# Routing of the second expert stage in groups of 1, 1, 1, 2 and 3 batches in place of 1, 1, 2, 2 and 2

## The chip, the cores and the metric
The kernel runs on one core of one Trainium2 chip. The time is device microseconds of one execution. Of the kernel before there are three: 1153.13, 1153.15 and 1154.1 us, median 1153.15 us. A further execution was recorded by the profiler.

## The reference, cut to what matters
The input x has 8 batches of 512 tokens with 128 channels, so 4096 tokens. Four layers follow each other, each added to x:

```
x = x + attention(layernorm(x))
x = x + experts(layernorm(x))        # first expert stage
x = x + delta_rule(layernorm(x))
x = x + experts(layernorm(x))        # second expert stage: the change is here
```

The experts are eight networks 128 -> 512 -> 128 with a GELU. Each token is sent to one of them:

```
logits = (x @ w_red) @ normalised(wg).T       # 8 numbers per token
idx    = argmax(softmax(logits)); score = softmax(logits)[idx]
out    = (gelu(x @ w1[idx] + b1[idx]) @ w2[idx] + b2[idx]) * score
```

## The kernel before, in words
x stays in SBUF as 32 tiles of 128 tokens x 128 channels, four tiles to a batch. The function `experts(..., f)` is built twice, with f = 0 and f = 1. In the second one (f = 1) it does the routing for all eight batches first, and only then the expert networks.

Routing sorts the tokens by expert. Each token's normalised row (with its own number behind it, 129 words) is written by an indirect DMA to a row of `xs_dram`, in the area of its expert. Its place there is the number of tokens that chose the same expert before it. The work goes by groups of batches, `GROUPS`, of 1, 1, 2, 2 and 2 batches. For a group the steps are:

- `moments(b)`, DVE: mean and variance of the four tiles of a batch, 4 statistics and 4 aggregations.
- `variance(g)` DVE, `deviation(g)` ACT (square root), `deviation(g)` DVE (reciprocal and one correcting step): 1/deviation of all tiles of the group.
- `normalize(g)`, DVE: `xa` from `x`, one instruction per tile.
- `turn(b)`, PE: four transposes of `xa` to PSUM; `turned(b)`, ACT: the copy `rT` to SBUF; `logits(b)`, PE: for each tile a product with the gate's weights.
- `choose(g)`, DVE: five instructions, from the logits to the one-hot `oh`.
- `ranks(g)`, PE: counts the tokens of each expert before each token; it starts from the group before's totals, which `counted(g - 1)`, ACT, copies to `cnt`.
- `place(g)`, DVE: three instructions, to the whole-number places `pos`.
- GpSimd (POOL): one indirect DMA per tile, from L1430, as soon as `place(g)` is done; four for a batch.

The groups are tied to each other by the running totals. Each engine works off its own list in the order in which it is written: DVE's and ACT's orders are written out by hand, PE takes group by group all turns, then all logits, then the ranks.

Behind the last `place`, DVE computes the tables (`tables()`: which expert each of the 24 tiles of 256 rows has, and from which row it is read). From its first result (`end_done`) ACT issues eight fills of 129 KB (L1496), which put blank rows behind each expert's last token. From its last result (`texp_done`) SP loads the weights of the first three tiles (L1375 to L1381). Then SP waits until all scatters and all fills have landed, and loads the rows of the first tiles (`f_xs`, L1390). The waits are these:

```
            for q in range(SLOTS - 1):
                weights(0, q, f > 0)
            sp.wait_ge(s["scat_done"], 16 * TT * (B // 2 + 1) + 16 * NT * f)
            sp.wait_ge(s["scat_odd"], 16 * TT * (B // 2 - 1))
            sp.wait_ge(s["fill_done"], 16 * E * (f + 1))
```

After that PE works through 24 tiles (transpose L1782, up L1792, down L1802, transpose back L1813), POOL scatters the results (L1438), SP loads them back in token order (L1413), and DVE adds them to x (L1717).

Of the kernel before, what the change touches and what calls it, by code (L numbers as in the profile page):

```python
# [14 lines left out]
B, T, C = 8, 512, 128  # L15
H, HD = 16, 8
TT = T // P
NT = B * TT
# [25 lines left out]
NC2 = ST // P  # L44
EPS_G = 1e-4
GROUPS = ((0, 1), (1, 2), (2, 4), (4, 6), (6, B))
SINGLE = tuple((b, b + 1) for b in range(B))
AREA = B * T + ST
IDLE = 2 * SPAN
# [1224 lines left out]
def experts(nc, x, xs_dram, ys_dram, s, keep, f, w_red, wg, w1, b1, w2, b2, out):  # L1274
    with ExitStack() as ctx:
# [18 lines left out]
        area = keep["area"]  # L1294
        tile_at = keep["tile_at"]
        k_at = keep["k_at"]
        GR = GROUPS if f else SINGLE
        NG = len(GR)
        FIRST = 0 if f else NG - 1
        GB, CB = B * f, (B - 1) * f  # L1300
# [49 lines left out]
        def tiles(g):  # L1350

            return slice(TT * GR[g][0], TT * GR[g][1])

        def width(g):

            return TT * (GR[g][1] - GR[g][0])

# [88 lines left out]
        def _(act):  # L1446
            def deviation(g):
                act.wait_ge(s["rstd_step"], 6 * (GB + g) + 1)
                if f == 0:
                    act.activation(rstd[:, 2, tiles(g)], rstd[:, 1, tiles(g)], ACT.Ln).then_inc(s["rstd_step"], 1)  # L1450
                    act.wait_ge(s["rstd_step"], 6 * (GB + g) + 2)
                    act.activation(rstd[:, 3, tiles(g)], rstd[:, 2, tiles(g)], ACT.Exp, scale=-0.5)\
                        .then_inc(s["rstd_step"], 1)
                else:
                    act.activation(rstd[:, 2, tiles(g)], rstd[:, 1, tiles(g)], ACT.Sqrt).then_inc(s["rstd_step"], 1)

            def turned(b):
                act.wait_ge(s["rT_ps"], B * f + b + 1)
                if b >= 2:
                    act.wait_ge(s["lg_ps"], B * f + b - 1)  # L1460
                act.activation(rT[:, b % 2, :], (bA, bB)[b % 2][:, :], ACT.Copy).then_inc(s["rT_sb"], 1)

            def counted(g):
                n = width(g)
                act.wait_ge(s["rank_ps"], GB + g + 1)
                act.activation(cnt[:, g % 2, :], rank_bank(g)[:, E * n:E * n + E], ACT.Copy).then_inc(s["cnt_sb"], 1)

            if f == 0:
                deviation(NG - 1)
                turned(B - 1)  # L1470
            else:
                deviation(0)
                turned(0)
                deviation(1)
                counted(0)
                turned(1)
                counted(1)
                deviation(2)
                turned(2)
                turned(3)  # L1480
                deviation(3)
                counted(2)
                turned(4)
                turned(5)
                deviation(4)
                counted(3)
                turned(6)
                turned(7)
            act.wait_ge(s["lg_step"], 4 * (GB + NG))
# [41 lines left out]
        def _(dve):  # L1531
            def moments(b):
                n0 = 2 * NT * f + 2 * TT * b
                four = range(TT * b, TT * b + TT)
                for i in four:
                    dve.bn_stats(stats[:, i, :], x[:, i, :]).then_inc(s["stat_done"], 1)  # L1536
                for k, i in enumerate(four):
                    dve.wait_ge(s["stat_done"], n0 + k + 1)
                    dve.bn_aggr(mv[:, i, :], stats[:, i, :]).then_inc(s["stat_done"], 1)

            def variance(g):
                dve.wait_ge(s["stat_done"], 2 * NT * f + 2 * TT * GR[g][1])
                dve.tensor_scalar(rstd[:, 1, tiles(g)], mv[:, tiles(g), 1], EPS_LN, None, ALU.add)\
                    .then_inc(s["rstd_step"], 1)
# [14 lines left out]
                dve.wait_ge(s["rstd_step"], n0 + 6)  # L1559
                dve.tensor_tensor(rstd[:, 0, at], rstd[:, 2, at], rstd[:, 3, at], ALU.mult).then_inc(s["rstd_ready"], 1)  # L1560

            def normalize(g):
                dve.wait_ge(s["rstd_ready"], GB + g + 1)
                for i in range(NT)[tiles(g)]:
                    dve.tensor_scalar(xa[:, i, 0:C], x[:, i, :], mv[:, i, 0:1], rstd[:, 0, i:i + 1],  # L1565
                                      ALU.subtract, ALU.mult).then_inc(s["xnf_done"], 1)

            def choose(g):

                at, n, n0 = tiles(g), width(g), 4 * (GB + g)  # L1570
                lg = bH[:, g % 4, 0:E * n].rearrange("p (i e) -> p i e", e=E)
                dve.wait_ge(s["lg_ps"], B * f + GR[g][1])
                dve.tensor_reduce(top[:, at], lg, AX.X, ALU.max).then_inc(s["lg_step"], 1)
                dve.wait_ge(s["lg_step"], n0 + 1)
                dve.tensor_tensor(lgx[:, at, :], lg, top[:, at].unsqueeze(2).broadcast_to([P, n, E]), ALU.subtract)\
                    .then_inc(s["lg_step"], 1)
                dve.wait_ge(s["lg_step"], n0 + 2)
                dve.scalar_tensor_tensor(hit[:, at, :], lgx[:, at, :], 0.0,
                                         pref[:, :].unsqueeze(1).broadcast_to([P, n, E]), ALU.is_equal, ALU.mult)\
                    .then_inc(s["lg_step"], 1)  # L1580
                dve.wait_ge(s["lg_step"], n0 + 3)
                dve.tensor_reduce(first[:, at], hit[:, at, :], AX.X, ALU.max).then_inc(s["lg_step"], 1)
                dve.wait_ge(s["lg_step"], n0 + 4)
                dve.tensor_tensor(oh[:, at, :], pref[:, :].unsqueeze(1).broadcast_to([P, n, E]),
                                  first[:, at].unsqueeze(2).broadcast_to([P, n, E]), ALU.is_equal)\
                    .then_inc(s["oh_done"], 1)
# [51 lines left out]
            if f == 0:  # L1638
                moments(B - 1)
                variance(NG - 1)  # L1640
                deviation(NG - 1)
                normalize(NG - 1)
                choose(NG - 1)
                place(NG - 1)
            else:
                moments(0)
                variance(0)
                deviation(0)
                normalize(0)
                moments(1)  # L1650
                variance(1)
                deviation(1)
                choose(0)
                normalize(1)
                place(0)
                moments(2)
                choose(1)
                moments(3)
                variance(2)
                place(1)  # L1660
                deviation(2)
                normalize(2)
                moments(4)
                moments(5)
                variance(3)
                choose(2)
                place(2)
                deviation(3)
                normalize(3)
                moments(6)  # L1670
                moments(7)
                variance(4)
                choose(3)
                place(3)
                deviation(4)
                normalize(4)
                choose(4)
                place(4)
            tables()
# [1040 lines left out]
```

## Time and profile before

| what | value |
|---|---|
| median of the runs | 1153.15 us |
| profiled execution, its own time | 1146.83 us |
| its span, first to last instruction | 1145.0 us |
| PE busy | 851.1 us (74%) |
| DVE busy | 760.2 us (66%) |
| POOL busy | 562.0 us (49%) |
| ACT busy | 535.8 us (47%) |
| mean granted TensorE clock | 0.849 of full |

The span is the time between the first and the last instruction; the execution's own time has 1.83 us more around it. Busy shares are means over very different stages. All times of rows are microseconds from the span's start. The second expert stage begins at about 956.8.

### The profile page before, as it was taken

The page shows a single profiled execution, that of the slowest core. Times are in us where ns is not written, and L with a number is a line of the kernel's source. Part 1 is how long each engine was busy: PE and PEld are TensorE (multiplying, and loading weights), DVE is VectorE, ACT ScalarE, POOL GpSimd, SP SyncE. Part 2 cuts the span into 40 slices and gives each one's busy share as a digit, 9 for nine tenths or more (in the row PEclk, how much of TensorE's full clock was granted, in tenths as well). Part 3 has the DMA queues.
Part 4 walks back from the last instruction along what each step waited for, and adds up shares of the span by engine and source line. Part 5 has one row for each costly group of instructions (what it writes and reads, how often), then busy time and mean ns, then how long its engine had stood idle before and what let it go on. Part 6 is the DMA issues. An engine that isn't in the chain of part 4 may idle for free. (4 is left out here: it accounts for less than half of the span.)

```text
span 1145.0 us, 26725 instructions
## 1 busy us (share of the span) xinstructions
PE 851.1 (74%) x9326; PEld 632.7 (55%) x9326; DVE 760.2 (66%) x1722; ACT 535.8 (47%) x1219; POOL 562.0 (49%) x698
## 2 busy tenths in 40 slices
PE   3678888888888753999188999467867674629992
PEld 2455555555555542888124786156655563528881
DVE  7577687786877741223364889999999997512224
ACT  4577667586675721454055220255555531115450
POOL 4456557575665631445550010277777841533442
PEclk9998888797887965999688999878889886559996
DMA  5342241432414004566338400000020110155665
GB/s 162 112 157 91 68 159 41 134 98 70 159 41 134 9 14 139 168 202 187 100 58 109 74 1 0 0 1 0 0 73 0 37 38 7 40 157 163 196 195 165
DMA packets 129207, 101.80 MB, mean 89 GB/s; under 512 B 20640, under 2 KB 116832, under 8 KB 129056
## 3 DMA queue, kind: packets, MB, share of 16 engines
q1 hardware_dynamic: 120080, 87.27, 27.6%
q0 software_dynamic: 5120, 10.53, 2.6%
q10 hardware_dynamic: 3904, 2.61, 0.7%
q8 instruction: 68, 1.11, 0.4%
q14 instruction: 35, 0.29, 0.1%
HBM read 57.98 MB, written 35.45 MB: 82 GB/s over the span
## 5 line engine op out<-in xcount | busy, mean ns | idle before, releaser
L795 DVE TENSOR_SCALAR a_mag<-a_pS 128x1024 int32<-128x1024 int32 (+1 forms) x192 | 179.9, 949 | 66.6 <-PE a_pS L1154 65.7
L552 ACT ACTIVATE a_pw<-a_mag,a_eps_a 128x1024 f32<-128x1024 f32 (+1 forms) x192 | 175.0, 936 | 56.7 <-DVE a_mag L795 50.7
L1438 POOL DMA_INDIRECT ys_dram<-f_yo,f_who x96 | 92.1, 960 | 133.6 <-DVE f_yo L1703 116.9
L415 POOL TENSOR_TENSOR a_pw<-a_pw,a_decay 128x256 f32<-128x256 f32 x128 | 93.4, 730 | 105.2 <-ACT a_pw L552 104.5
L1154 PE MATMUL a_pS<-a_qf,a_kf 64*64 64x192 bf16 (+3 forms) x1536 | 112.2, 272 | 5.2 <-DVE a_mag L795 4.5
L1513 ACT ACTIVATE f_hs<-f_bH,f_bs 128x256 f32<-128x256 f32 x192 | 75.4, 475 | 69.0 <-PE f_bH L1792 69.0
L2613 PE MATMUL d_c<-d_pb_p,ident 128*128 128x256 f32 x256 | 72.3, 452 | 42.1 <-POOL d_pb_p L2096 42.1
L1186 PE MATMUL a_pOff<-a_pw,a_vo 128*18 128x64 f32 x3584 | 95.9, 241 | 1.2 <-issue 1.2
L1792 PE MATMUL f_bH<-f_xsT,f_w1s 128*128 128x256 f32 x384 | 95.6, 394 | 0.0
L1688 DVE TENSOR_SCALAR f_ysT<-f_bY,f_bs 128x256 f32<-128x256 f32 x48 | 23.2, 483 | 108.2 <-PE f_bY L1802 108.2
L1802 PE MATMUL f_bY<-f_hs,f_w2s 128*128 128x256 f32 x384 | 90.8, 379 | 0.0
L2613 PEld LDWEIGHTS d_c<-d_pb_p,ident 128*128 128x128 f32 x256 | 58.5, 232 | 56.3 <-issue 40.8
L1154 PEld LDWEIGHTS a_pS<-a_qf,a_kf 64*64 64x64 bf16 x1536 | 65.8, 116 | 30.7 <-DVE a_mag L795 7.6
L2613 PE MATMUL d_c<-d_pb_d,ident 128*128 128x256 f32 (+1 forms) x256 | 64.6, 419 | 21.7 <-POOL d_pb_d L2096 21.7
L2090 POOL TENSOR_TENSOR d_pb_p<-d_Q,d_s_sb 128x512 f32<-128x512 f32 x32 | 37.5, 1171 | 83.1 <-ACT d_s_sb L2198 83.1
L1186 PEld LDWEIGHTS a_pOff<-a_pw,a_vo 128*18 128x18 f32 x3584 | 68.6, 110 | 15.9 <-issue 11.4
L1792 PEld LDWEIGHTS f_bH<-f_xsT,f_w1s 128*128 128x128 f32 x384 | 72.4, 199 | 8.9
L1802 PEld LDWEIGHTS f_bY<-f_hs,f_w2s 128*128 128x128 f32 x384 | 69.4, 190 | 7.5
L2613 PEld LDWEIGHTS d_c<-d_pb_d,ident 128*128 128x128 f32 x256 | 53.1, 220 | 33.1 <-POOL d_pb_d L2096 24.6
L363 POOL TENSOR_TENSOR a_vo<-a_vd,a_reach 128x1008 f32<-128x1008 f32 (+6 forms) x56 | 66.0, 1194 | 1.1 <-issue 1.1
L1703 DVE COPY f_yo<-f_bO 128x256 f32<-128x256 f32 x48 | 20.4, 425 | 62.0 <-PE f_bO L1813 62.0
L2194 ACT ACTIVATE d_G<-d_c,d_g_ahead 128x64 f32<-128x64 f32 x64 | 24.1, 376 | 71.2 <-DVE d_og L2431 71.2
(395 smaller groups left out, 1837.9 us busy)
## 6 DMA issues: line engine op xcount, KB each, us to landing
parts_scratch<-a_parts SPq DMA_DIRECT2D x32, 384.0 KB, 3.4
f_w1s<-in_L_ffn_w_dram SPq DMA_DIRECT2D x48, 256.0 KB
f_w2s<-in_L_ffn_w_dram SPq DMA_DIRECT2D x48, 256.0 KB
a_kf<-parts_scratch SPq DMA_DIRECT2D x16, 512.0 KB, 4.8
a_qf<-parts_scratch SPq DMA_DIRECT2D x16, 512.0 KB, 5.6
f_xs<-xs_dram SPq DMA_DIRECT2D x48, 129.0 KB, 2.3
parts_scratch<-a_parts SPq DMA_DIRECT2D x16, 256.0 KB, 2.4
xs_dram<-blank ACTq DMA_DIRECT2D x16, 129.0 KB, 4.2
```

The lines of the kernel that those rows point to most:

```text
L363: pool.tensor_tensor(vo[:, vo_at(j, j + 1):vo_at(j, j + 1) + n, :, :], vd[:, k, j, :, :].unsqueeze(1).broadcast_to([P, n, NP, 18]), reach[ ...
L415: pool.tensor_tensor(own, own, decay[:, k, m, hf:NP:2, :], ALU.mult)\
L552: act.activation(pw[:, n % 4, 0:N], mag[:, n % 3, 0:N], ACT.Square, bias=eps_a[:, 0:1])\
L795: dve.tensor_scalar(mag[:, n % 3, 0:2 * N].bitcast(I32).rearrange("p (l t) -> p l t", l=2), pS[:, 2 * (n % 2):2 * (n % 2) + 2, 0:N].bitcas ...
L1154: ins = pe.matmul(pS[lo:hi, 2 * (n % 2) + Q // 2, at:at + L * (end - first)], kf[lo:hi, k, p, L * m:L * m + L], qf[lo:hi, k, p, L * first: ...
L1186: ins = pe.matmul(pOff[lo:hi, L * i:L * i + L], vo[:, vo_at(m, i), p, :], wi, start=False, stop=(m == NM - 2), skip_group_check=True)
L1438: pool.indirect_dma_start(ys_dram[f][:, :], bass.IndirectOffsetOnAxis(ap=who[:, q, a:a + 1], axis=0), yo[:, q, a, :], None).then_inc(ys_ou ...
L1513: ins = act.activation(hs[:, q % 2, n, :], bH[:, 2 * (q % 2) + n // 2, ST * (n % 2):ST * (n % 2) + ST], ACT.Gelu, bias=bs[:, q, n:n + 1])
L1792: ins = pe.matmul(bH[:, 2 * (q % 2) + n // 2, ST * (n % 2):ST * (n % 2) + ST], w1s[:, q, P * n:P * n + P], xsT[:, q % 2, :], start=True, s ...
L1802: ins = pe.matmul(bY[:, 0:ST], w2s[:, q, n, :], hs[:, q % 2, n, :], start=(n == 0), stop=(n == NF - 1))
L2090: pool.tensor_tensor(po[:, 0:8], Q[:, :, :, bass.ds(c, 1)].rearrange("p k j c -> p k (j c)").unsqueeze(3) .broadcast_to([P, HD, CH, HD]), ...
L2613: ins = pe.matmul((c5, c6)[a][:, 0:64 * chunks].rearrange("p (c x) -> p c x", x=64), ident[:, :], po[:, k], start=(k == 0), stop=(k == 15))
```

## The change
The second expert stage takes its groups from a new tuple. `normalize` gets a batch beside the group. The batches of a group are normalised one at a time, some before and some after the `place` of the group before it. The orders on DVE and ACT are rewritten for it. The first expert stage still has a single batch here, and does the same instructions as before.

```
+ROUTED = ((0, 1), (1, 2), (2, 3), (3, 5), (5, B))
-        GR = GROUPS if f else SINGLE
+        GR = ROUTED if f else SINGLE
ACT, from the third deviation on:
                 turned(1)
+                deviation(2)
                 counted(1)
-                deviation(2)
                 turned(2)
-                turned(3)
                 deviation(3)
                 counted(2)
+                turned(3)
                 turned(4)
-                turned(5)
                 deviation(4)
                 counted(3)
+                turned(5)
                 turned(6)
                 turned(7)
DVE:
-            def normalize(g):
+            def normalize(g, b):
                 dve.wait_ge(s["rstd_ready"], GB + g + 1)
-                for i in range(NT)[tiles(g)]:
+                for i in range(TT * b, TT * b + TT):
...
                 moments(2)
+                variance(2)
                 choose(1)
+                deviation(2)
+                normalize(2, 2)
+                place(1)
                 moments(3)
-                variance(2)
-                place(1)
-                deviation(2)
-                normalize(2)
                 moments(4)
-                moments(5)
                 variance(3)
                 choose(2)
+                deviation(3)
+                normalize(3, 3)
                 place(2)
-                deviation(3)
-                normalize(3)
+                normalize(3, 4)
+                moments(5)
                 moments(6)
                 moments(7)
                 variance(4)
                 choose(3)
+                deviation(4)
+                normalize(4, 5)
                 place(3)
-                deviation(4)
-                normalize(4)
+                normalize(4, 6)
+                normalize(4, 7)
                 choose(4)
                 place(4)
```

## Rows read from the trace of the kernel before

**Rows 1.** Chain of waits, routing's end to the kernel's end: start, us, what
```profile
1009.56 14.37 issue
1023.93 0.67 PE f_bA L1782 x2
...
1025.15 0.66 PE f_bA L1782 x2
...
1116.42 1.73 PE f_bH L1792 x8
```

**Rows 2.** Waits of SP's queue: who waited for what, total us, times, longest
```profile
SPq L1397 <- DMA xs_dram<-blank: 3.3, 1, 3.3
SPq L1386 <- DMA xs_dram<-f_xa,f_pos: 0.4, 1, 0.4
```

**Rows 3.** Timeline of SP and ACT, after the last places: start, us, instruction
```profile
1007.00 8.25 ACTq L1496 DMA_DIRECT2D xs_dram<-blank  x8
...
1016.56 0.62 SPq L1381 DMA_DIRECT2D f_bs<-bT  x1
1021.73 1.57 SPq L1390 DMA_DIRECT2D f_xs<-xs_dram  x2
```

**Rows 4.** Timeline of POOL, first and last scatter of the last group
```profile
1006.08 0.96 POOL L1430 DMA_INDIRECT xs_dram<-f_xa,f_pos  x1 [0.94 <-DVE f_pos L1599]
...
1014.94 0.96 POOL L1430 DMA_INDIRECT xs_dram<-f_xa,f_pos  x1 [0.30 <-issue]
```

**Rows 5.** Line L1430, all 32 scatters of the stage: duration ns min/median/max, first and last start
```profile
L1430 POOL DMA_INDIRECT xs_dram<-f_xa,f_pos x32: 956/962/1095, 968.1 to 1014.9; - x32
```

**Rows 6.** Busy time by stretch: us, busy by engine, clock, DMA share, GB/s
```profile
1015.00:1016.00 1.00, 0.00 (x0) 0.00 (x0) 0.00 (x0) 0.00 (x0) 0.90 (x1) 0.50 0.96 260
...
1019.00:1020.00 1.00, 0.00 (x0) 0.00 (x0) 0.00 (x0) 0.00 (x0) 0.00 (x0) 0.50 0.73 200
...
1021.00:1022.00 1.00, 0.00 (x0) 0.00 (x0) 0.00 (x0) 0.00 (x0) 0.00 (x0) 0.50 0.04 7
```

**Rows 7.** Timeline of DVE, groups of one batch
```profile
959.41 1.11 DVE L1565 TENSOR_SCALAR f_xa<-x,f_mv,f_rstd 128x128 f32<-128x128 f32 x4
...
964.30 0.19 DVE L1573 TENSOR_REDUCE f_top<-f_bH 128x4 f32<-128x32 f32 x1 [0.87 <-PE f_bH L1738]
...
970.18 0.19 DVE L1573 TENSOR_REDUCE f_top<-f_bH 128x4 f32<-128x32 f32 x1 [1.88 <-PE f_bH L1738]
...
972.95 0.17 DVE L1599 CAST f_pos<-f_pos_f 128x4 int32<-128x4 f32 x1
```

**Rows 8.** Timeline of DVE, fourth group (two batches) and its places
```profile
991.62 0.22 DVE L1573 TENSOR_REDUCE f_top<-f_bH 128x8 f32<-128x64 f32 x1 [2.13 <-PE f_bH L1738]
...
994.36 0.23 DVE L1595 TENSOR_TENSOR f_p_at<-f_bO,f_oh 128x64 f32<-128x64 f32 x1 [1.50 <-ACT cnt L1466]
...
994.96 0.20 DVE L1551 RECIPROCAL f_rstd<-f_rstd 128x8 f32<-128x8 f32 x1
...
996.00 2.14 DVE L1565 TENSOR_SCALAR f_xa<-x,f_mv,f_rstd 128x128 f32<-128x128 f32 x8
1002.65 0.22 DVE L1573 TENSOR_REDUCE f_top<-f_bH 128x8 f32<-128x64 f32 x1 [4.51 <-PE f_bH L1738]
...
1005.63 0.17 DVE L1599 CAST f_pos<-f_pos_f 128x8 int32<-128x8 f32 x1
```

**Rows 9.** Timeline of PE: logits and ranks
```profile
965.44 0.64 PE L1752 MATMUL f_bY<-area,one_row 1*128 1x40 f32 x2 [1.18 <-DVE f_oh L1584]
...
988.15 3.43 PE L1738 MATMUL f_bH<-w_gate,f_rT 128*128 128x8 f32 x16
```

**Rows 10.** Busy time by stretch: last two groups; then the expert networks' first microseconds
```profile
990.00:1003.00 13.00, 8.15 (x43) 7.31 (x42) 4.97 (x23) 2.66 (x4) 9.11 (x11) 0.50 0.15 48
...
1030.00:1031.00 1.00, 1.00 (x6) 0.84 (x5) 0.00 (x0) 1.00 (x4) 0.00 (x0) 0.86 0.00 0
```

**Rows 11.** Result scatters of the expert networks (L1438): us to landing
```profile
DMA to landing us min/median/max: 2.2/2.6/3.6
```

## What the change will do to the time: the prediction
> **What bounds the kernel now.** I read the chain of waits first, then the waits of SP, then the timelines of the second expert stage. The chain shows that from 1023.93 us on PE works almost without a pause to 1116.42 + 1.73 = 1118.15, and that before it stand 14.37 us, from 1009.56, in which no engine computes anything on the path [rows 1]. The output part behind it is not touched. So whatever moves the first row load at 1021.73 [rows 3] moves the end by as much; the routing counts only through it.
>
> The reader should ask what that first row load waited for. SP was through with the weights at 1016.56 + 0.62 = 1017.18 [rows 3]. Then it waited 3.3 us for the last fill, to 1020.5, and after that another 0.4 us for a scatter [rows 2]. So the last scatter landed at about 1020.9, and the load followed 0.85 us later (1021.73 - 1020.9). Fill and scatter were nearly equally late. The last scatter had started on POOL at 1014.94 [rows 4], so it took L = 6.0 us to land. The result scatters of the same kind, of nearly equal size, take 2.2 at best, 2.6 in the median and 3.6 at most [rows 11]. The 6.0 has a reason in view: weights, fills and scatters run together, the DMA engines are at 0.96 of their time and more at 1015, still at 0.73 at 1019, and at 0.04 once the last of it is in, at 1021 [rows 6].
>
> **What the change does, part by part.** I call F the time by which the last `place` ends earlier; before, it ends at 1005.63 + 0.17 = 1005.80 [rows 8]. Number of instructions: one batch's tiles keep the same number of statistics, normalisations, transposes and logits. There are still five groups, so `choose`, `place`, `ranks`, `deviation` keep their number too; only their widths differ. All of the gain is order: a group's chain DVE, ACT, PE, DVE no longer waits for the normalisation of two batches at once, and DVE's idle time before `choose` is used once less.
>
> The path after the change, from the first place where it differs:
>
> - `choose(1)` starts at 970.18 as before [rows 7]: the new `variance(2)` lies in front of it, in the 1.88 us in which DVE waits for the logits [rows 7]. So this edit costs nothing; without that cover it would cost 0.2.
> - `choose` with four tiles lasts 1.14 (964.30 to the ranks on PE at 965.44) [rows 7, 9], `deviation` 1.04 (994.96 to 996.00), from the reciprocal to the normalisation [rows 8], one batch's normalisation 1.11 [rows 7]. From 970.18 that gives 973.45 for the normalised batch 2. Its square root lies beside `choose(1)`.
> - From the end of a single normalisation (959.41 + 1.11 = 960.52) to `choose` are 3.78 us [rows 7]: `choose(2)` at 977.25. Moments of batches 3 and 4 and `variance(3)`, some 2.4 us, lie inside these 3.8.
> - `choose(2)` 1.14, `deviation(3)` 1.04, batch 3's normalisation 1.03 (half of 2.14, less the tail), `place(2)` 0.60 (994.36 to 994.96) [rows 8], batch 4's normalisation 1.11: 982.2. From the end of a pair's normalisation (996.00 + 2.14) to `choose` are 4.51 us [rows 8]: `choose(3)` at 986.7.
> - `choose(3)` with eight tiles 1.3 (five instructions of 0.22 in place of 0.19) [rows 7, 8], `deviation(4)` 1.04, batch 5 1.03, `place(3)` 0.60, batches 6 and 7 2.14: 992.8. `place(3)` here waits for the counts, which PE and ACT make under the deviation and batch 5's normalisation.
> - Then 4.51 as for a pair, and one batch's logits more, half of 3.43 = 1.7 [rows 9]: `choose(4)` at 999.0.
> - From `choose` to the end of `place`: with eight tiles in the last group 3.15 (1002.65 to 1005.80). Eight tiles cost about 0.5 more than four: 3.34 from 991.62 to the instruction behind the last of `place` at 994.96, against 2.94 from 970.18 to 972.95 + 0.17, and that end lies some 0.1 later than the other [rows 7, 8]. So twelve 3.65: the last `place` ends at 1002.65.
>
> That makes F = 3.15. The steps on DVE are each taken to the end of the last instruction or to the start of another engine's; the next instruction on DVE itself starts a few hundredths earlier. An estimate of 0.04 for each of the eleven handovers gives 3.6. I take **F = 3.3**.
>
> What the change takes back: the last group has 12 scatters in place of 8. Eight take 1014.94 - 1006.08 = 8.86 from the first start to the last, 1.266 each [rows 4], so four more put the last start 5.06 us further behind the last `place`. POOL must be free by then: the fourth group's places end at about 990.6 (992.8 less the 2.14), its eight scatters take 10.1 to 1001.0, and the first of the last group is ready at 1002.5 + 0.28 = 1002.8. It is free, by 1.8 us. The last scatter thus starts at 1014.94 - 3.3 + 5.06 = 1016.7, **later than before by 1.8 us**.
>
> What then goes with F: tables, fills and weights all hang on the last `place`, so the fills that landed at 1020.5 land at about 1017.2, plus what four scatters more in that stretch cost them. A scatter moves 128 rows of 129 words, 66 KB; at the 260 GB/s of this stretch [rows 6] that is 0.25 us, 1.0 for four. So the fills are in by 1018.2 at the latest, and are no longer last. And the DMA engines run empty before the last scatter needs them: the tail that ended at 1021.1 ends at 1017.8 to 1018.8. The last scatter therefore lands after L = 2.2 to 3.6 [rows 11]. I take the median, 2.6, since some tail is left. Row load: 1016.7 + 2.6 + 0.85 = 1020.15 against 1021.73. In one formula, the row load comes earlier by F - 5.06 + (6.0 - L) = 3.3 - 5.06 + 3.4 = **1.6 us**. Bounds: with L = 2.2 and F = 3.6, 2.3 earlier; with L = 3.6 and F = 3.15, 0.5 earlier; with L = 6.0, 1.8 later. The sum for the profiled execution, 1146.83 with a span of 1145.0, is 1145.2. The median of the runs is 6.3 above the profiled one, and I move it by the same difference: 1153.15 - 1.6 = 1151.5.
>
> On L the trace's shortest is 2.2 [rows 11]. The Trainium skill, "DMA: Bandwidth & Descriptors", section "Anatomy of one DMA", gives a DMA from GpSimd a fixed 2.0 us, mostly the receipt of the write, and bytes by 436 GB/s: an estimate of 2.15 us for 66 KB. The trace's 2.2 agrees; its 6.0 under full load does not follow from that rule. By it the sum would be 2.05 us, and 1151.1.
>
> A cost that I put at nothing: the normalisations of batches 6 and 7 now run on DVE while POOL issues the fourth group's scatters. The 32 scatters last 956 to 1095 ns, with the median at 962, although many of them already lie beside normalisations [rows 5]. So I see no loss; even 0.2 us for each of eight would not use up the 1.8 us by which POOL is free. The Trainium skill, "SBUF — State Buffer", section "SBUF: two separate sides", says that certain DVE instructions lock GpSimd out of a shared port, so that it can't write the descriptors of its DMAs. That would speak against this order; the durations of this trace do not show it.
>
> **Rivals.**
>
> A. The forecast: 1.6 us earlier, 1151.5. For it: the load's last two waits end within 0.4 us of each other, and both come with full DMA engines [rows 2, 6].
>
> B. The scatter tail decides on the other side. The landing time stays at 6.0, because the twelve scatters' packets still queue behind weights and fills, with 0.26 MB more to move. Then POOL's 5.06 us outweigh F: 1.8 us later, 1154.9. It decides from L = 4.2 on (5.06 - 3.3 = 1.8 less than 6.0). For it: 6.0 is the only number for this spot. Against: the engines are nearly idle by 1021 [rows 6], and everything else moves forward.
>
> C. The front gains less than the steps say: the chain through PE, ACT and DVE has four handovers with new neighbours, and DVE may be late for `choose(4)`. With F = 0 and L = 2.6 the load is 1.7 later: 1154.8. The break is at F = 1.7. Against: DVE has 4.51 us of idle time before the last `choose` [rows 8] and the terms are all measured.
>
> D. TensorE's clock rises in the last group. Routing runs at 0.50, that is 1.2 GHz, from 990 to 1003 [rows 10]. In the expert networks PE runs unbroken from 1025.15 [rows 1], and the granted clock rises within 1030 to 1031 (mean 0.86) [rows 10], some 5.1 us later. The new last group keeps PE at work from about 990 to 999. If the clock doubled at about 996, the rest of the logits and the ranks would take half: 1.5 us less, so 3.1 earlier in all, 1150.0. Against: 997 to 1002.6 was also nearly unbroken and stayed at 0.50, with logits of only eight columns [rows 8 to 10].
>
> That the change does nothing isn't a case: the orders are different on three engines. That all of F arrives (1149.8) is ruled out by POOL: the last scatter can't be in before 1016.7 + 2.2.
>
> **How the numbers follow.** A 0.62, B 0.12, C 0.12, D 0.08, and 0.06 for gains or losses of the later stage's clock that I can't place. The likeliest is A: 1151.5; its own range is 1150.4 to 1152.8. The range to 8 in 10 takes in part of B, C and D: 1149.7 to 1154.6. A difference can be told from no change only beyond 0.2%, 2.3 us. A lies mostly within it; a third of A, nearly all of D and half of the rest are faster than that: 0.20 + 0.07 + 0.03 = 0.30. B and C are slower by less than 2.3 in most of their course; a third of their 0.24 and a little of the rest are slower than that: 0.10. The same: 0.60.
>
> **What would show it.** In the changed kernel: last `place` ends at 1002.2 to 1002.7; last scatter starts at 1016.3 to 1017 and POOL idles between the fourth and last group; SP's longest wait after the weights is for a scatter and no longer for a fill; the first row load is at 1019.5 to 1020.9; PE's granted clock is 0.50 in all of the routing. A scatter that lands after more than 4.2 us proves B, a last `place` after 1004.1 proves C, a clock above 0.50 before 1003 proves D. The forecast is wrong if the row load moves by the amount said and the end doesn't.

## The result, and the profile after

The changed kernel takes 1150.68 us in the median of 17 runs (1149.16 to 1154.53), the kernel before 1153.68 in the median of 17 runs beside them (1151.43 to 1156.16). The ratio is 0.9976 with a 95% interval of 0.9966 to 0.9985, that is 2.8 us faster (1.7 to 3.9). Run again twice beside the experiments, the same kernel gave 0.9968 and 0.9970, so 3.7 and 3.5 us. The forecast was 1.6 us faster, with 1149.7 to 1154.6 as the range. The sign was right and the time lies in the range; 1.6 itself lies just below the measured interval, and one term of the sum was well off.

The profiled execution of the changed kernel has 1151.33 us of its own (span 1149.5), 0.65 above its median. That of before had 1146.83, which is 6.3 to 6.9 us *below* the median of its runs. So the two profiles can't be set beside each other as they stand: the changed kernel's is 4.5 us longer although the kernel is faster. Of these 4.5 us, 2.8 are there before the second expert stage begins (959.61 against 956.78), in code that the change does not touch, and 2.1 come behind the first row load (125.4 us to the end of the span against 123.3). I therefore took two more profiles of the kernel before, unchanged, and compare with them too.

The second expert stage starts with the first statistics on DVE. Here that row, before and then after (timeline of DVE; start, us, instruction, in brackets the idle time before it and what ended it). All times "into the stage" below are counted from it: 956.78 before, 959.61 after.

```profile
956.78 0.87 DVE L1536 BATCH_NORM_STATS2 f_stats<-x 128x6 f32<-128x128 f32 x4 [0.32 <-PEq L1839]
```

After, timeline of DVE: `choose` of groups 2, 3 and 4 (L1574) and the last place (L1596, L1600).

```profile
959.61 0.87 DVE L1537 BATCH_NORM_STATS2 f_stats<-x 128x6 f32<-128x128 f32 x4 [0.32 <-PEq L1843]
...
979.90 0.19 DVE L1574 TENSOR_REDUCE f_top<-f_bH 128x4 f32<-128x32 f32 x1 [0.77 <-PE f_bH L1742]
...
989.53 0.23 DVE L1574 TENSOR_REDUCE f_top<-f_bH 128x8 f32<-128x64 f32 x1 [1.55 <-PE f_bH L1742]
...
1001.73 0.26 DVE L1574 TENSOR_REDUCE f_top<-f_bH 128x12 f32<-128x96 f32 x1 [6.15 <-PE f_bH L1742]
...
1005.13 0.26 DVE L1596 TENSOR_TENSOR f_p_at<-f_bY,f_oh 128x96 f32<-128x96 f32 x1 [1.98 <-PE f_bY L1761]
...
1005.71 0.17 DVE L1600 CAST f_pos<-f_pos_f 128x12 int32<-128x12 f32 x1
```

These answer to [rows 8]. The three `choose` are 20.29, 29.92 and 42.12 us into the stage; the prediction had 20.47, 29.92 and 42.22. The last place ends at 1005.71 + 0.17 = 1005.88, 46.27 into the stage, where before it was 1005.80 - 956.78 = 49.02: 2.75 earlier, forecast 3.3.

Part of the missing half microsecond shows in the last ranks. Timeline of PE: they end at 1003.95 + 0.74 = 1004.69, and DVE goes on at 1005.13, 0.44 later. On most handovers of this stage that gap is 0.04.

```profile
1003.95 0.74 PE L1761 MATMUL f_bY<-f_oh,ones 128*128 128x96 bf16 x12
```

After, timeline of POOL, first and last scatter of the last group, answering to [rows 4]: POOL was idle for 2.60 us before the last group (0.94 before) and starts the last scatter 60.43 into the stage.

```profile
1006.16 0.96 POOL L1431 DMA_INDIRECT xs_dram<-f_xa,f_pos  x1 [2.60 <-DVE f_pos L1600]
...
1020.04 0.96 POOL L1431 DMA_INDIRECT xs_dram<-f_xa,f_pos  x1 [0.31 <-issue]
```

After, timeline of ACT and SP, answering to [rows 3]: the eight fills, then the DMAs of the weights, then the first row load.

```profile
1007.09 11.90 ACTq L1497 DMA_DIRECT2D xs_dram<-blank  x8
...
1016.87 0.01 SPq L1382 DMA_DIRECT2D f_bs<-bT  x1
...
1023.31 0.01 SPq L1382 DMA_DIRECT2D f_bs<-bT  x1
1024.12 2.75 SPq L1391 DMA_DIRECT2D f_xs<-xs_dram  x3
```

Nobody had forecast this. Before, SP was through with the weights at 1017.18, 60.40 into the stage, and waited 3.7 us more. After, it sends the last of the weights only at 1023.31, 63.70 in, and the row load follows 0.81 later without any wait for a fill or a scatter. The chain of waits names SP's own instructions there (start, us, what):

```profile
1017.57 0.70 SPq L1373
1018.27 0.69 issue
```

What takes 0.7 us is, each time, a single small instruction. The rows of the weights' line show it, first before, then after (durations in ns min/median/max, first and last start). The same MOVE lasts 45 at most in the one and 700 in the other; the fills on ACT last 11.90 in place of 8.25. I call these hold-ups.

```profile
L1375 SPq MOVE f_w1s<-in_L_ffn_w_dram x3: 29/29/45, 1010.3 to 1015.4; - x3
```

```profile
L1376 SPq MOVE f_w1s<-in_L_ffn_w_dram x3: 5/45/700, 1010.4 to 1020.4; - x3
```

Then the two kernels' row loads: 64.95 into the stage before, 64.52 after. By these two profiles the change would bring 0.4 us. The median says 2.8.

### The profile page after: what moved, and what is told of

The parts are those of the page before. It is cut to its first block and busy times, and to the rows that moved or that the text cites. A ratio compares the mean times of both kernels' runs of the same rounds, so it can differ in the third digit from the quotient of the medians.

```text
span 1149.5 us, 26726 instructions
## 1 busy us (share of the span) xinstructions
PE 853.0 (74%) x9326; PEld 630.0 (55%) x9326; DVE 761.6 (66%) x1722; ACT 536.1 (47%) x1219; POOL 560.9 (49%) x698
```

## The experiments

Each time is the median of its runs, each ratio against the kernel before in the same job. That kernel's median was 1153.32 (27 runs) for the first four, 1155.63 (23) for the next four, 1156.92 (29) for the last four.

**The change again**, three profiles in all with the one further down. No edit.

> The changed kernel once more, for a second profile of it and its time beside the next three on the same chip. In its first profile the stage starts at 959.61 us in place of 956.78, before anything that the change touches, so all times are taken from the stage's start (its first statistics on DVE). My theory, that the last place comes about 3 us earlier and the last scatter lands in under 4.2 us: first row load 62 to 64 us after the stage's start (before: 64.95), time 1.5 to 3 us under the kernel before. Rival, that POOL's longer last group gives the time back: row load at 65 or later and no gain. In the first profile SP and ACT had single instructions of 0.7 us while the weights were issued; if that belongs to the change it comes again, if it is chance it is gone.

1149.40, ratio 0.9968 (0.9954 to 0.9982), so 3.7 us faster (2.1 to 5.3), more than expected. The profiled execution took 1153.71, 4.3 above that median. Its row load, 64.72 us into the stage, lies between what was expected (62 to 64) and the rival (65 or later), and the hold-ups came again: the fills last 11.22 us. SP waited for a scatter now, and shortly (waits of SP: who for whom, total, times, longest; then the timeline of SP; the stage starts at 960.09 here):

```profile
SPq L1387 <- DMA xs_dram<-f_xa,f_pos: 0.3, 1, 0.3
```

```profile
1024.81 2.75 SPq L1391 DMA_DIRECT2D f_xs<-xs_dram  x3
```

**Only the order**: groups 1, 1, 2, 2, 2 as before, but rows normalised batch by batch around the places. In the third group, for instance (against the changed kernel):

```
-ROUTED = ((0, 1), (1, 2), (2, 3), (3, 5), (5, B))
+ROUTED = ((0, 1), (1, 2), (2, 4), (4, 6), (6, B))
...
+                variance(2)
                 deviation(2)
                 normalize(2, 2)
                 place(1)
+                normalize(2, 3)
```

> Only the order is changed: groups of 1, 1, 2, 2 and 2 batches as before, but of each pair one batch is normalised before the place of the group in front and one behind it. Steps from the rows of before: last place 2.7 us earlier; POOL has no idle time left before the last eight scatters, so its last scatter starts only 0.6 us earlier. Theory 1 (the backlog of weights, fills and scatters on the DMA engines sets the row load, all of which hangs on the last place): about 2.5 us faster, as much as the whole change, so the new groups add nothing. Theory 2 (POOL's last scatter plus a fixed 6 us sets it): 0.6 us faster.

1154.17, ratio 1.0014 (0.9998 to 1.0030): both expectations missed. The profiled execution took 1161.13, 7.0 above that median, so its row load is not the usual one. Timelines of PE, ACT, POOL, DVE and SP (the stage starts at 960.21; the 15.94 are the eight fills):

```profile
996.40 0.45 PE L1761 MATMUL f_bO<-f_oh,ones 128*128 128x64 bf16 x8
1000.14 0.18 ACT L1467 ACTIVATE cnt<-f_bO 128x8 f32<-128x8 f32 x1 [8.02 <-remote]
1001.38 0.96 POOL L1431 DMA_INDIRECT xs_dram<-f_xa,f_pos  x1 [2.76 <-DVE f_pos L1600]
...
1010.37 0.17 DVE L1600 CAST f_pos<-f_pos_f 128x8 int32<-128x8 f32 x1
1011.75 15.94 ACTq L1497 DMA_DIRECT2D xs_dram<-blank  x8
...
1032.09 2.75 SPq L1391 DMA_DIRECT2D f_xs<-xs_dram  x3
```

The fourth group's ranks end at 996.85, and ACT, which makes the counts from them, starts only at 1000.14: a pause of 3.29 us in which ACT does nothing and everything that needs the counts stands, POOL too. The last place ends 50.33 into the stage instead of near 46, and the row load is at 71.88. The pause does not explain that row load: the last scatter starts at 60.16 and has landed at 62.47, and what holds the load are the fills, which are issued over 15.94 us (8.25 in the first profile of before) and land at 71.03. So this profile shows why the last place missed its mark, but not why the median shows no gain.

**Only the groups**: 1, 1, 1, 2, 3, but each group normalised in one piece behind the place, as before. In the last group, for instance (against the changed kernel):

```
 ROUTED = ((0, 1), (1, 2), (2, 3), (3, 5), (5, B))
...
                 choose(3)
+                place(3)
                 deviation(4)
                 normalize(4, 5)
-                place(3)
                 normalize(4, 6)
                 normalize(4, 7)
```

> Only the groups are changed: 1, 1, 1, 2 and 3 batches, and each group is normalised in one piece behind the place of the group in front, as in the kernel before. Steps from the rows: last place 0.8 us later than before, last scatter starts 5.8 us later, so with a landing in 2.6 us the row load and the time are 2.4 us later than before. If the groups were what gives the gain, it would be faster by 1 us or more.

1154.40, ratio 1.0007 (0.9996 to 1.0019). No gain, but not the loss of 2.4 us that was expected. Timeline of PE, DVE and SP (the stage starts at 956.68):

```profile
997.88 5.12 PE L1742 MATMUL f_bH<-w_gate,f_rT 128*128 128x8 f32 x24
...
1004.38 0.26 DVE L1574 TENSOR_REDUCE f_top<-f_bH 128x12 f32<-128x96 f32 x1 [7.46 <-PE f_bH L1742]
...
1007.96 0.17 DVE L1600 CAST f_pos<-f_pos_f 128x12 int32<-128x12 f32 x1
1026.13 2.75 SPq L1391 DMA_DIRECT2D f_xs<-xs_dram  x3
```

Here too a pause: the last logits end at 1003.00, DVE goes on at 1004.38, 1.38 later. The last place ends at 51.45, and the row load is at 69.45; in the usual execution of before (below) they are near 52.3 and 68.9.

**Four groups**: 1, 2, 2, 3, batch by batch as in the change; the orders on DVE and ACT follow.

```
-ROUTED = ((0, 1), (1, 2), (2, 3), (3, 5), (5, B))
+ROUTED = ((0, 1), (1, 3), (3, 5), (5, B))
```

> Four groups of 1, 2, 2 and 3 batches, normalised batch by batch around the places: one whole pass through the chain of engines less. Steps from the rows: last place 7.9 us earlier than before, POOL's last scatter starts 2.9 us earlier (POOL is busy almost without a gap from the second group on). If the chain's passes and POOL's queue are what counts, with a landing of 2.6 us: about 6 us faster than before. If the landing stays at 6 us: 2.7 us faster. If the routing's end doesn't matter: no difference.

1146.99, ratio 0.9951 (0.9936 to 0.9966): 5.7 us (3.9 to 7.4) faster than before, as expected, and the lowest ratio but one here (0.9950 with late weights, below, is the same within the noise). The same timelines (the stage starts at 955.39):

```profile
996.49 0.26 DVE L1572 TENSOR_REDUCE f_top<-f_bH 128x12 f32<-128x96 f32 x1 [6.59 <-PE f_bH L1736]
...
1000.07 0.17 DVE L1598 CAST f_pos<-f_pos_f 128x12 int32<-128x12 f32 x1
1018.13 2.75 SPq L1391 DMA_DIRECT2D f_xs<-xs_dram  x3
```

Last place at 44.85, row load at 62.74. The steps of the expectation were counted from the first profile of before and missed: the last place was to come 7.9 us earlier and comes 4.2 earlier. Here too there is a long pause, 3.28 us between the third group's ranks and ACT's counts, and the kernel is fast all the same.

**The kernel before, twice more**, one execution each. No edit.

> The kernel before, profiled once more. All five profiles of other kernels so far, the change's two among them, show single instructions of SP and ACT of 0.7 us, in the weights' issue and in the first expert stage too, whose code is the same; the one profile of the kernel before shows none. If that is a state of the execution and not of the change, this profile shows them too, and its first row load comes 2 us or more later than the 64.95 us after the stage's start of the first profile. If it belongs to the changed order, this profile shows none and 65 us again.

> The kernel before, third profile. Its last place was at 49.0, 52.2 and, with four more scatters behind it, 53.1 us after the stage's start. If the short one was the exception: 52 to 53 again, with a pause between PE's logits or ranks of the fourth and fifth group and the engine that waits for them. If the pauses are chance: 49 to 50.

1155.67 and 1157.43 us, 0.04 and 0.5 above the medians of that kernel in their jobs (1155.63 and 1156.92). I call these two the usual execution of before. Timelines of PE, DVE, POOL and SP, of the first (the stage starts at 959.70):

```profile
1009.20 0.45 PE L1757 MATMUL f_bY<-f_oh,ones 128*128 128x64 bf16 x8
1011.17 0.22 DVE L1595 TENSOR_TENSOR f_p_at<-f_bY,f_oh 128x64 f32<-128x64 f32 x1 [2.70 <-remote]
...
1011.69 0.17 DVE L1599 CAST f_pos<-f_pos_f 128x8 int32<-128x8 f32 x1
1020.99 0.96 POOL L1430 DMA_INDIRECT xs_dram<-f_xa,f_pos  x1 [0.30 <-issue]
...
1028.29 1.57 SPq L1390 DMA_DIRECT2D f_xs<-xs_dram  x2
```

and of the second (the stage starts at 958.41):

```profile
989.79 3.44 PE L1738 MATMUL f_bH<-w_gate,f_rT 128*128 128x8 f32 x16
995.18 0.23 DVE L1573 TENSOR_REDUCE f_top<-f_bH 128x8 f32<-128x64 f32 x1 [4.04 <-remote]
...
1010.75 0.17 DVE L1599 CAST f_pos<-f_pos_f 128x8 int32<-128x8 f32 x1
...
1027.66 2.75 SPq L1390 DMA_DIRECT2D f_xs<-xs_dram  x3
```

In the first, the last ranks end at 1009.65 and DVE goes on at 1011.17, 1.52 later; in the second, the fourth group's logits end at 993.23 and `choose` starts at 995.18, 1.95 later. The last place ends 52.16 and 52.51 into the stage, not 49.02, and the row load is at 68.59 and 69.25, not 64.95. Every later profile of this order has both pauses (the two experiments on it below: 53.13 and 53.18). So the profile that the forecast was made from is the one of five without them. All thirteen later profiles, of whatever kernel, have hold-ups somewhere in the expert stages; in that one the longest MOVE, register or semaphore instruction of SP and ACT there lasts 186 ns. In both of the two more profiles SP's only wait behind the weights is for a fill, 2.6 and 2.5 us; the last scatter has landed 0.3 us before it. The row of the first:

```profile
SPq L1397 <- DMA xs_dram<-blank: 2.6, 1, 2.6
```

**Four more scatters behind the last group**, into a buffer that nothing reads, once in the changed kernel and once in that of before; SP waits for them as for the others.

```
+            for i in range(NT - TT, NT) if f else ():
+                pool.indirect_dma_start(more_dram[:, :], ..., xa[:, i, :], None).then_inc(s["scat_done"], 16)
...
-            sp.wait_ge(s["scat_done"], ... + 16 * NT * f)
+            sp.wait_ge(s["scat_done"], ... + 16 * (NT + TT) * f)
```

> The changed kernel with four more scatters behind the last group's twelve: the last batch's rows once more, into a buffer that nobody reads, and the wait for the scatters counts them. If POOL's last scatter sets the first row load (my prediction's A), it comes 5.06 us later than in the changed kernel, and the time is 4 to 5 us above it. If the issue of the weights on SP, or the fills, set it, the scatters have slack and the time rises by less than 2 us.

> The same four more scatters in the kernel before, so its last group has twelve as in the changed one, with nothing else changed. My prediction's formula with F = 0: the last scatter starts 5.06 us later but lands in 2.6 us and no longer in 6.0, so 1.7 us slower. If the landing stays at 6 us: 5 us slower. If the weights' issue on SP sets the row load: no change.

In the changed kernel 1155.09, ratio 0.9992 (0.9979 to 1.0005), which is 1.8 to 2.8 us above what the changed kernel gave in the three comparisons (0.9968 to 0.9976), with an uncertainty of about 2. That is between the two expectations (4 to 5, or under 2). In that of before 1157.41, ratio 1.0022 (1.0008 to 1.0037), 2.6 us slower (0.9 to 4.3): between the 1.7 of the forecast's formula and the 5 of a landing that stays at 6. Timeline of POOL and SP in the changed kernel (the stage starts at 960.02):

```profile
1023.63 0.00 SPq L1383 DMA_DIRECT2D f_bs<-bT  x1
1025.48 0.96 POOL L1435 DMA_INDIRECT more_dram<-f_xa,f_pos  x1 [0.30 <-issue]
1029.26 2.36 SPq L1392 DMA_DIRECT2D f_xs<-xs_dram  x3
```

POOL's last scatter is 5.0 later than in the change, and the row load, at 69.24, is 3.8 to 4.7 later than in its three profiles; the last weights are issued 5.6 us before it. So POOL's tail is the bound once it is 5 us longer, though the time follows by some half of it only. In the kernel before with four more, the last scatter lands 3.5 us after its start and the row load is at 71.62, 2.4 to 3.0 later than in the usual execution, and there the time follows one to one.

**The weights later**: of the last three tiles' weights, only the first is loaded ahead of the row loads; the others are issued behind the first and the second row load. Once on the change, once on the four groups, once on the kernel before.

```
-            for q in range(SLOTS - 1):
+            for q in range(1 if f else SLOTS - 1):
...
+                if f and q:
+                    weights(0, q, f > 0)
```

> The changed kernel, in which SP issues the weights of the second and third tile only behind the first and second row load. If SP's issue of the weights sets the first row load, that load comes earlier, by at most what the weights of two tiles take there, and the kernel is faster than the changed one by 1 to 3 us. If POOL's last scatter sets it, the load moves only by what the emptier DMA engines give the scatter's landing (up to 1 us), and the later weights may cost as much: no difference beyond 1 us.

1149.87, ratio 0.9950 (0.9934 to 0.9966), against 0.9976, 0.9968 and 0.9970 of the change without it: 2.1 to 3.0 us better, but with an uncertainty of 2.2 to 2.4 and not in one job, so a gain is likely and not shown. Timelines of ACT, POOL and SP (the stage starts at 956.74):

```profile
1004.21 8.14 ACTq L1499 DMA_DIRECT2D xs_dram<-blank  x8
...
1017.17 0.95 POOL L1433 DMA_INDIRECT xs_dram<-f_xa,f_pos  x1 [0.30 <-issue]
...
1020.34 1.57 SPq L1391 DMA_DIRECT2D f_xs<-xs_dram  x2
```

The fills last 8.14 again. SP waits 7.5 us for them, to 1016.97, and then for the last scatter: its next instruction (L1387) starts only at 1019.47. POOL ends where it ended, 60.43 into the stage, and the row load is at 63.60 instead of 64.52. The scatter landed 2.15 us after its start.

> Both edits that gained: groups of 1, 2, 2 and 3 batches, and the weights of the second and third tile only behind the first row loads. With four groups the last scatter starts 1.4 us earlier after the stage's start than in the changed kernel (59.04 against 60.4), and with the late weights the load follows it by 3.2 us: first row load at 62.2, time 3 to 5 us under the changed kernel. If the two gains are one and the same (both only shorten SP's part), it is no faster than the better of the two alone, some 6 us under the kernel before.

1151.63, ratio 0.9961 (0.9946 to 0.9975), beside 0.9970 (0.9956 to 0.9984) of the change alone in the same job:

> The changed kernel again, beside the three others on the same chip. If the pauses of PE's results are tied to the order of the instructions, this third profile shows the last place at 46.2 to 46.3 again, as the four profiles with this order did, and the time is 0.2 to 0.35% under the kernel before. If they are chance, the last place is at 47 to 50 here.

So 3 to 5 us were expected and 1.0 came, with an uncertainty of about 2.3. In its profile the row load is at 1018.45 - 956.26 = 62.19, only 0.55 before that of the four groups alone, so no sign that the gains add; but that execution, 1147.27, is the shortest of its twelve, 4.4 below their median, and may not be the usual one. The change alone took 1153.97 in this job; in its profile SP did wait for the last scatter (waits; then POOL and SP, the stage starts at 960.28):

```profile
SPq L1387 <- DMA xs_dram<-f_xa,f_pos: 1.5, 1, 1.5
```

```profile
1020.74 0.96 POOL L1431 DMA_INDIRECT xs_dram<-f_xa,f_pos  x1 [0.30 <-issue]
...
1025.77 2.75 SPq L1391 DMA_DIRECT2D f_xs<-xs_dram  x3
```

The landing is 1025.77 - 0.85 - 1020.74 = 4.2 us here.

> The kernel before with the late weights. It has eight scatters in the last group, so its row load follows the last place by some 13 us, where the changed kernel with late weights needs 17.3 (46.3 to 63.6). If PE's results come without pauses (last place at 49), the row load is at 62 and the change gains nothing with late weights; if the pauses of the second profile (last place at 52.2 and 53.1) are the usual case, it is at 65 to 66 and the changed kernel with late weights is 1.5 to 2.5 us faster. Against the kernel before it should gain 2 to 4 us, since SP's issue and the fills are shorter.

1156.01, ratio 0.9991 (0.9977 to 1.0005): no difference that can be told, where 2 to 4 us had been expected. In its profile SP waited 7.2 us for a fill, the last scatter landed 0.2 us after the last fill, and the row load is at 67.72, about 1.2 earlier than in the two profiles of before.

## Why the prediction was right, and which term was off

The row load, in us into the stage, with what lies ahead of it:

| | last place ends | last scatter starts | last weights issued | row load | own time |
|---|---|---|---|---|---|
| before, first profile | 49.02 | 58.16 | 59.78 | 64.95 | 1146.83 |
| before, two more | 52.16, 52.51 | 61.29, 61.63 | 64.38, 65.44 | 68.59, 69.25 | 1155.67, 1157.43 |
| after, three profiles | 46.27, 46.21, 46.31 | 60.43, 60.40, 60.46 | 63.70, 62.93, 61.74 | 64.52, 64.72, 65.49 | 1151.33, 1153.71, 1155.87 |

Against the usual executions of before, the row load comes 68.9 - 64.9 = 4.0 us earlier. That is to be compared with 1.6 forecast and with 2.8 (1.7 to 3.9), 3.7 and 3.5 measured in time. Beside the one profile that the forecast was made from, it comes 0.4 us earlier: the last scatter starts 2.3 us later (1.8 was said), it lands 3.4 us sooner after its start (as said), and SP needs 1.5 us from the landing to the load instead of 0.8, since it is still issuing weights.

1. **The front, F = 3.3: the mis-sized term.** The steps themselves held: `choose(2)`, `choose(3)` and `choose(4)` within 0.2 us. What they left out are pauses between PE's recorded end and the engine that waits for it. They add up to 0.7 to 1.0 at the fourth group's logits and in the last group of the change, and to over 3 in the usual execution of before. So F is (52.16 + 52.51) / 2 - 46.26 = 6.1, not 3.3. Of it, 2.75 is what the forecast had argued (each engine waits for less), and 3.3 are the pauses of before's usual execution (last place near 52.3 against 49.0 in its first profile), whose cause is open. Without those 3.3 the same sum, 2.75 - 5.06 + 2.8 (point 3), brings the row load only about half a microsecond earlier, so most of the gain rests on a part that nobody forecast. The forecast took it from the one execution in which both the pauses and the hold-ups were missing. The sign of that was on the page: its own time was 6.3 us below the median of the runs. The prediction noted its own time and did not draw the conclusion.
2. **POOL's take-back, 5.06: right.** 6.1 - 5.06 leaves 1.0, and the last scatter starts 61.5 - 60.4 = 1.0 earlier. That the tail gains least was the forecast's core, and it held.
3. **The landing, 6.0 down to 2.6: right in kind.** The traces hold the moment of each landing. From the start of the last scatter it is 6.0 in the first profile of before and 6.2 and 6.4 in the two more; in the change it is 2.6, 3.5 and 4.2. It is 2.1 with four more scatters and 2.15 with late weights. The means give 6.3 - 3.5 = 2.8 us; 3.4 had been said. In the five microseconds behind the last scatter the DMA engines' share is 0.99 to 1.14 in the usual execution of before (1022 to 1027, first of the two); in the change's first profile it is 0.57 to 0.79 (1021 to 1024). The Trainium skill, "DMA: Bandwidth & Descriptors", section "Anatomy of one DMA", gave an estimate of 2.15 us; the 2.15 with late weights agrees, the 3.5 and 4.2 beside weights and fills don't follow from that rule. The 1.0 of point 2 and this term make up the 4.0, to 0.2.
4. **"SP's longest wait is for a scatter, no longer for a fill": half right.** No fill was waited for in any of the three profiles. The scatter was waited for 0, 0.3 and 1.5 us. In the first, what was last was SP's own issue of weights, held up in small instructions, a case the prediction did not have. Issue and scatter tail are nearly equal: with the weights later the load moves by 0.9 and then stands at the scatter.
5. **The normalisations beside scatters cost nothing: right.** The scatters keep their length (line L1431, all 36 recorded, durations in ns):

```profile
L1431 POOL DMA_INDIRECT xs_dram<-f_xa,f_pos x36: 954/958/1095, 433.1 to 1020.0; - x36
```

6. **The rivals.** B (landing stays at 6.0) fell: 2.6 to 4.2. The third profile's 4.2 stands at the very limit that the prediction had set for B, and the kernel was still 3.5 us faster in that job: the limit went with F = 3.3, and with F = 6.1 even 6.0 would have left a gain. C (F lost) fell: the last place is at 46.2 to 46.3 in all of five profiles with this order, the two experiments that keep it included. D (clock rises in the routing) fell: the granted clock is 0.50 in every stretch from 960 to 1007, the last group's logits among them, after (busy by engine, granted clock, DMA share, GB/s):

```profile
1000.00:1003.00 3.00, 1.69 (x8) 1.60 (x8) 1.13 (x5) 0.38 (x2) 2.31 (x3) 0.50 0.20 63
```

7. **The signs, and what is luck.** Counted into the stage, the prediction named 45.4 to 45.9 for the last place, 59.5 to 60.2 for the last scatter and 62.7 to 64.1 for the row load. In all three profiles each came later: 46.2 to 46.3, 60.4 to 60.5, 64.5 to 65.5. Put F = 6.1 into its formula and it gives 6.1 - 5.06 + 3.4 = 4.4, above the interval of the main comparison. That the forecast's 1.6 came as near as it did is in part luck: the F that was too small, and the premise that the end moves by as much as the row load, which did not hold in full (below), pull in opposite directions.

**What does it, order or groups?** Neither by itself. The order alone gives 1.0014 and the groups alone 1.0007, both together 0.9968, in one job. In both halves a long pause stands where none was expected (3.29 and 1.38 us), so what they tell is that the gain needs both *as timed here*, and not that either part alone would be worth nothing without those pauses. For the order alone even this is open, since its one profile is of an execution 7.0 us above the median. The four groups show the argument further on: one group less, the last place 1.4 earlier with as many scatters behind it, the row load 64.52 - 62.74 = 1.8 earlier, and 1149.40 - 1146.99 = 2.4 us less in time.

**What stays open.** Why a pause comes at one handover and not at another. Several return at the same place, with nearly the same length, in the later profiles of one order; but the first profile of before has that order and none of them, so the order alone does not decide. That the delay is real for those who wait is shown, since ACT, POOL and the last place are late by it, and the waiting engine is not what is slow: with the order alone, PE's signal is recorded at 1000.12, 3.27 us after the recorded end of the ranks, and ACT starts 0.02 later. No run tells whether the matmul ended later than recorded or its signal came late. The profiles of the experiments come from three chips; on which the first one of before was taken is not on record, so a difference between chips is not ruled out for it. The cause of the hold-ups is not shown either, only that with the weights issued later the fills last 8.1 us in all three profiles. And the time does not follow the row load one to one: from the row load to the end of the span it is 123.3 us in the first profile of before and 125.4 to 128.2 in the thirteen others. TensorE's clock is likely a part of it: with the change's first profile it stands at 0.50 at 1029 to 1030 and at 1.00 from 1031, 3.8 us after the first matmul (1026.30); in the second profile of the same kernel it is still 0.50 at 1032 to 1033, with the first matmul at 1027.12. Windows of the one and the other:

```profile
1029.00:1030.00 1.00, 1.00 (x4) 0.81 (x3) 0.00 (x0) 0.00 (x0) 0.00 (x0) 0.50 0.87 292
1030.00:1031.00 1.00, 1.00 (x6) 0.78 (x6) 0.00 (x0) 0.01 (x1) 0.00 (x0) 0.93 0.81 217
```

```profile
1032.00:1033.00 1.00, 1.00 (x4) 0.78 (x4) 0.00 (x0) 0.55 (x2) 0.00 (x0) 0.50 0.25 72
1034.00:1035.00 1.00, 1.00 (x6) 0.90 (x5) 0.00 (x0) 0.30 (x2) 0.00 (x0) 1.00 0.00 0
```

So two executions of one kernel differ by some 2.7 us in the time from the first matmul to full speed, while their row loads differ by 0.2. Their own times are 1151.33 and 1153.71.

## What to carry to other kernels

Before pricing anything from a profile, hold its own time against the median of the runs: where it is half a per cent off, its waits may not be the usual ones, and a forecast of a few microseconds made from it can be off by as much. The same holds for the profile of an experiment. A wait at the end of a chain is the maximum of several queues (here fills, weights' issue, scatters and their landing); price each of them after the change, the issuing engine itself too, and expect the second to be late next. Regrouping pays where the front's gain exceeds the longer tail behind it, here 6.1 against 5.1, more than half of the 6.1 by pauses that went away unplanned; the rest came from a last scatter that landed sooner.

## What the runs showed of the hardware that I had not expected

- An engine that waits for PE goes on 0.04 us after the recorded end of the matmul on most handovers, but 0.2 to 3.3 us after it on a few. They go with the order of instructions, though not with it alone: 1.52 to 1.57 at the last ranks of before's order in four profiles of five and 0.04 in the fifth; 3.28 or 3.29 at one group's ranks in the order alone and in both kernels of four groups.
- SP's and ACT's small instructions around a DMA, 17 to 186 ns long in the first profile of before, take about 700 ns now and then while POOL's indirect DMAs, SP's weights and ACT's fills are issued together. In the change's first profile three of them stand among the fills, which last 11.90 us in place of 8.25, and six on SP up to the row load, whose weights end 3.3 us later. In the thirteen profiles 280 such instructions of the expert stages last over 400 ns; 211 begin while an indirect DMA of POOL runs and 273 within 0.35 us of one. That is a coincidence in time and no cause shown.
- Four scatters more behind the last group moved the row load by 3.8 to 4.7 us and the time by 1.8 to 2.8 in the changed kernel; in the kernel before by 2.4 to 3.0, and the time by 2.6 (0.9 to 4.3).
